# A Mamba block with a mixture of experts on one core: halves of channels added on GpSimd ahead of mean and variance, a reordered prologue, and a last store in two halves

## The chip, the cores and the metric

The kernel runs on one core of one Trainium2 chip. The metric is the device time of one execution in microseconds (us). Five engines work side by side and meet at semaphores: TensorE (PE in the profile), VectorE (DVE), ScalarE (ACT), GpSimd (POOL) and SyncE (SP, which only issues the DMAs here).

## What is computed

Four sequences of 256 positions with 256 channels go through two layers. Both are residual:

```python
x = x + ssm(ctx_1024, layernorm(x), ...)      # conv of 4 taps, silu, softplus, a scan over 256
                                              # positions with 16 states, gate silu(z)
x = x + ffn(layernorm(x), ...)
# in ffn, for all 1024 positions:
shared_out = sum(expert_apply(flat, w1, b1, w2, b2) for 2 shared experts) / 2
probs      = softmax(flat @ router_w + router_b)           # 32 experts, the 6 largest kept
routed_out = sum(g_e * expert_apply(flat, w1_e, b1_e, w2_e, b2_e) for all 32 experts)
# expert_apply: relu(x @ w1 + b1) @ w2 + b2, hidden width 176
# layernorm: (x - m) / sqrt(v + 1e-5), m and v over the 256 channels
```

All tensors are float32. The gates of experts that were not chosen are zero, so the kernel runs all 32 experts over all positions and multiplies by the gate.

## The kernel before

**Tiling.** A batch is one sequence, b = 0 to 3. Channels lie on the partitions in KD = 2 halves of 128 (k = 0, 1), positions along the free axis (L = 256). The hidden width of all experts is cut into NT = 47 tiles of 128 rows, taken in NP = 24 pairs (PAIRS; pair 1 is a single tile). For a pair the first layer is `z` (L546 to L548, twelve matmuls of two fp32r pieces each way), ScalarE applies bias and relu (L678), VectorE multiplies by the gate (`hg`, L853; L855 for the shared experts), and the second layer adds w2 times hg into the PSUM bank `acc` (L527), SKEW = 3 pairs later. In the profile an fp32 matmul leaves two records: "x8" at L527 is four matmuls. In batch 3 `hg` and w2 are split in two fp32r pieces (`split`), and the second layer of a pair is twelve matmuls.

**Staging.** While the 24 pairs of batch b run, the steps in front of and behind the scan of batch b+1 (table THIS) and the convolution, x_proj and dt of batch b+2 (table NEXT) are woven in. A table says beside which pair a step is issued; each engine goes through its own steps in the order of the pairs. On PE a step comes between the pair's first-layer matmuls and its second-layer matmuls, or behind the latter if its name is in BEHIND. The loop over batches is a hardware loop (Fori) for the first two, then written out. In front of pair 0 of batch 0 stands the prologue HEAD, a list of steps that every engine walks in this order and of which it takes its own. OPEN holds the steps beside pairs 0, 1 and 2 of batch 0.

**The steps that matter here.** `warm` is PE alone: n matmuls over a tile of ones (L448), some of them after a semaphore. `xin` (PE, L458), `cv0` (ACT), `taps` (DVE, L722; the range of taps stands in the name), `econv` (ACT), `uclip` (DVE), `usig` (ACT, two activations) and `u` (DVE, L738) give the convolved input u. `xall` is x_proj on PE (L467), written to `xdt`, which is the bank `dA[0]`; `dtl` (ACT, L605) copies it to `xd`, SP spills it to DRAM and loads it back spread over the partitions (`bc`, `bt`, `ct`); `dt` (PE), `sp` (ACT), `over`, `delta` (DVE) give the step width. Then come per state and half k: `bu` (POOL, L905), `decay` (ACT), `scan` and `prod` (DVE, L753 and L766), `fold` (POOL) or, in the prologue, `sum` (PE, L436, into `acc`). `ez1` to `ez3` (ACT) and `zmul` (DVE, L784) give the gate silu(z) in `sz`. `x1` (DVE, L794 to L799) is the residual. The second layernorm is `mean` (PE, L479: two matmuls with a matrix of 1/256, one for each half k, summed in PSUM), `centre` (DVE, L802), `sq` (ACT, L654), `var` (PE, L484, two matmuls), `r2` (ACT, L657 and L659), `norm` (DVE, L807 to L811, gives `xs`), `xh` (ACT) and `xl` (DVE) as its two pieces, `logits` (PE, L504), `top`, `ex`, `gates` (router) and `turn` (PE, L498, and ACT, L668: the gates transposed into `gT`). For batch 0 the gates of the first 16 experts are spread on chip: `spread` (PE, L490, into the bank `misc`; ACT, L665, copies it to `gt`). `w1h` (ACT, L574) and `w1l` (POOL, L888) split the first-layer weights in two pieces, in 12 chunks that SP loads into a ring of four (`stage`). `final` (DVE, L872) adds `acc` to the residual after a batch's last pair, and SP stores it (`store`, L352).

**Banks.** PSUM has z (4 banks), acc, dA[0], dA[1] and misc: all eight are in use. The transposed gates are written to misc, as is what `spread` writes; a copy out of misc has to be done before the next write.

```python
elif name == "turn":
    pe.wait_ge(S["g34_done"], b + 1)
    if first(b):
        pe.wait_ge(ld_g[0], 32)        # ACT's copy of the spread gates out of misc
```

## Time and profile before

| | us |
|---|---|
| median of 3 runs | 389.01 |
| the three runs | 388.66 to 389.68 |
| the profiled execution, as timed | 390.97 |
| its span in the trace | 389.2 |
| busy: PE / DVE / ACT / POOL | 360.5 / 260.1 / 216.8 / 196.2 |
| mean granted clock of TensorE | 0.968 of full |

The span runs from the first to the last event of the profiled execution. The granted clock is 1.00 or 0.50 for most stretches of the trace: 2.4 or 1.2 GHz. The time falls into a prologue (to about 66 us, with PE busy in part), the start of batch 0 (to about 93 us), and three and a half batches in which PE works without a pause, then the last store.

### The profile page before, as it was taken

The page shows a single profiled execution, that of the slowest core. Times are in us where ns is not written, and L with a number is a line of the kernel's source. Part 1 is how long each engine was busy: PE and PEld are TensorE (multiplying, and loading weights), DVE is VectorE, ACT ScalarE, POOL GpSimd, SP SyncE. Part 2 cuts the span into 40 slices and gives each one's busy share as a digit, 9 for nine tenths or more (in the row PEclk, how much of TensorE's full clock was granted, in tenths as well). Part 3 has the DMA queues.
Part 4 walks back from the last instruction along what each step waited for, and adds up shares of the span by engine and source line. Part 5 has one row for each costly group of instructions (what it writes and reads, how often), then busy time and mean ns, then how long its engine had stood idle before and what let it go on. Part 6 is the DMA issues. An engine that isn't in the chain of part 4 may idle for free.

```text
span 389.2 us, 6828 instructions
## 1 busy us (share of the span) xinstructions
PE 360.5 (93%) x2275; PEld 321.3 (83%) x2275; DVE 260.1 (67%) x449; ACT 216.8 (56%) x539; POOL 196.2 (50%) x152
## 2 busy tenths in 40 slices
PE   4646688899999999999999999999999999999996
PEld 2333466688999988999999889989999999999995
DVE  3379987579998547799877566799864534354443
ACT  2667765657764426477543445485523346565662
POOL 0479996078995002389852002799730024445442
PEclk9659899899999999999999999999999999999999
DMA  7397870169622324886322125974231244233320
GB/s 232 114 319 253 252 229 7 47 177 315 202 83 81 83 57 111 247 308 183 113 81 81 54 92 149 325 220 145 90 83 56 67 131 144 82 85 91 100 56 27
DMA packets 30735, 54.20 MB, mean 139 GB/s; under 512 B 3282, under 2 KB 8564, under 8 KB 30708
## 3 DMA queue, kind: packets, MB, share of 16 engines
q1 hardware_dynamic: 30708, 53.86, 45.5%
q8 instruction: 14, 0.23, 0.3%
q14 instruction: 13, 0.11, 0.1%
...
## 4 chain that ended last, share of the span: by engine, by line
PE 82%; DVE 9%; DMA 3%; issue 3%; ACT 1%; POOL 1%; DVEq 0%; POOLq 0%; SPq 0%; ACTq 0%
PE acc L527 39%; PE z L546 12%; PE z L548 11%; PE z L547 11%; DVE dA L753 5%; DMA bt<-bc 2%; PE z L448 2%; PE dA L467 1%; DMA bc<-xd 1%; PE acc L436 1%; PE acc L532 1%; PE misc L484 1%; PE misc L458 1%; PE misc L479 1%; DVE ya L766 1%
## 5 line engine op out<-in xcount | busy, mean ns | idle before, releaser
L527 PE MATMUL acc<-hg,w 128*128 128x256 f32 x564 | 133.6, 379 | 0.3 <-DVE hg L853 0.3
L678 ACT ACTIVATE z<-z,par 128x256 f32<-128x256 f32 x188 | 76.0, 440 | 99.3 <-PE z L548 99.2
L905 POOL TENSOR_TENSOR bu<-bt,du 128x512 f32<-128x512 f32 x64 | 81.1, 1279 | 86.0 <-DMA bt<-bc 58.8
L546 PE MATMUL z<-xh,w1l 128*128 128x256 f32 (+1 forms) x376 | 119.0, 316 | 0.3 <-DVE xl L815 0.3
L527 PEld LDWEIGHTS acc<-hg,w 128*128 128x128 f32 x564 | 102.4, 190 | 11.6 <-DVE hg L853 0.5
L853 DVE TENSOR_TENSOR hg<-z,gt 128x512 f32<-128x512 f32 x88 | 60.5, 688 | 74.0 <-ACT z L678 73.1
L548 PE MATMUL z<-xh,w1h 128*128 128x256 f32 (+1 forms) x376 | 106.5, 283 | 0.0
L547 PE MATMUL z<-xl,w1h 128*128 128x256 f32 (+1 forms) x376 | 106.2, 283 | 0.0
L753 DVE TENSOR_TENSOR_SCAN dA<-dA,bu 128x512 f32<-128x512 f32 x64 | 78.2, 1222 | 9.9 <-POOL bu L905 9.4
L546 PEld LDWEIGHTS z<-xh,w1l 128*128 128x128 f32 x376 | 71.4, 190 | 6.7 <-issue 4.7
L547 PEld LDWEIGHTS z<-xl,w1h 128*128 128x128 f32 x376 | 71.0, 189 | 1.6
L548 PEld LDWEIGHTS z<-xh,w1h 128*128 128x128 f32 x376 | 70.9, 189 | 0.0
L913 POOL TENSOR_TENSOR ya<-ya,pr 128x512 f32<-128x512 f32 x42 | 53.9, 1282 | 22.7 <-DVE pr L766 22.0
L926 POOL TENSOR_TENSOR w2l<-w,w2h 128x512 fp32r<-128x512 f32 (+1 forms) x24 | 31.3, 1304 | 64.1 <-ACT w2h L685 64.1
L626 ACT ACTIVATE dA<-delta,aneg 128x255 f32<-128x255 f32 x128 | 55.0, 462 | 0.0
L766 DVE TENSOR_TENSOR pr<-dA,ct 128x512 f32<-128x512 f32 x50 | 34.6, 692 | 6.1 <-DVE dA L753 0.5
L888 POOL TENSOR_TENSOR w1l<-stage,w1h 128x1024 fp32r<-128x1024 f32 (+1 forms) x12 | 27.5, 2323 | 13.9 <-ACT w1h L574 13.9
L623 ACT ACTIVATE dA<-zeros 128x2 f32<-128x2 f32 x64 | 11.1, 173 | 36.7 <-DVE pr L766 27.8
L527 PE MATMUL acc<-hh,w2h 128*128 128x256 f32 x94 | 26.5, 282 | 0.0
L527 PE MATMUL acc<-hh,w2l 128*128 128x256 f32 x94 | 26.5, 282 | 0.0
L527 PE MATMUL acc<-hl,w2h 128*128 128x256 f32 x94 | 26.4, 281 | 0.0
L436 PE MATMUL acc<-pr,par 128*128 128x256 f32 x32 | 10.7, 475 | 11.1 <-DVE pr L766 11.1
...
## 6 DMA issues: line engine op xcount, KB each, us to landing
w<-in_w SPq DMA_DIRECT2D x92, 256.0 KB, 2.8
bt<-bc SPq DMA_DIRECT2D x32, 256.0 KB, 4.9
ct<-bc SPq DMA_DIRECT2D x32, 256.0 KB, 5.6
...
gt<-gates SPq DMA_DIRECT2D x14, 128.0 KB
xr<-in_xr SPq DMA_DIRECT2D x4, 256.0 KB, 5.7
x<-in_xT SPq DMA_DIRECT2D x4, 256.0 KB, 4.3
out<-x SPq DMA_DIRECT2D x4, 256.0 KB, 4.7
```

What stands on the lines that cost most here:

```text
L527: mm = pe.matmul(acc[:, k, :], weights, h, start=t + k + n == 0, stop=last, skip_group_check=True)
L546: pe.matmul(z[p % ZB][:, i, :], w1l[:, t, one], xh_, start=k == 0, stop=False)
L547: pe.matmul(z[p % ZB][:, i, :], w1h[:, t, one], xl_, start=False, stop=False)
L548: mm = pe.matmul(z[p % ZB][:, i, :], w1h[:, t, one], xh_, start=False, stop=k == KD - 1)
L626: ins = act.activation(dA[k][:, j, 1:L], delta[:, k, 1:L], ACT.Exp, scale=aneg[:, n:n + 1])
L678: ins = act.activation(z[p % ZB][:, i, :], z[p % ZB][:, i, :], ACT.Relu, bias=b1[:, t:t + 1])
L753: dve.tensor_tensor_scan(flat(dA[k]), flat(dA[k]), bu[:, (c * KD + k) % BURING, :], 0.0, ALU.mult, ALU.add).then_inc(S["scan_done"], 1)
L766: dve.tensor_tensor(products(b, c)[:, k, :], flat(dA[k]), flat(ct[:, c % BRING]), ALU.mult).then_inc(S["prod_done"], 1)
L853: ins = dve.tensor_tensor(hg[:, p % 4], z[p % ZB][:], gt[:, 2 * half:2 * half + 2, :], ALU.mult)
L905: pool.tensor_tensor(bu[:, r, :].rearrange("p (j l) -> p j l", j=2), bt[:, c % BRING], du[:, k:k + 1, :].broadcast_to([P, 2, L]), ALU.mult ...
L913: pool.tensor_tensor(ya[:, k, :], ya[:, k, :], pr[:, k, :], ALU.add).then_inc(S["y_folded"], 1)
L926: pool.tensor_tensor(w2l[:, p % 4, 0:n, :], w2[:, p % RING, 0:n, :], w2h[:, p % 4, 0:n, :].bitcast(F32), ALU.subtract).then_inc(S["w2l_don ...
```

## The change

It has six parts.

1. **Mean and variance, batches 1 to 3.** GpSimd adds the two channel halves of x1 (`x1s`, beside pair 18) and of the squares (`sqs`, beside pair 19) into free quarters of `ya`; `mean` and `var` are then one matmul each instead of two. `mean` moves from behind the second layer of pair 18 to ahead of that of pair 19; `var` moves from ahead of the second layer of pair 20 to behind it. Batch 0 keeps its two matmuls.
2. **Spread gates in acc.** `spread` writes to acc, which is free until the second layer of batch 0 begins, instead of misc; `turn` no longer waits for the copy; a new step `acc_free` has PE wait for the copy after the first layer of pair 2. `spread` and `turn` move from pair 2 to pair 1.
3. **x_proj of batch 1 ahead of pair 0.** `xall` and `dtl` move from behind pair 0 into the prologue, between the logits and pair 0; `dt`, `sp`, `over`, `delta` move from pair 1 to pair 0. On the way `taps`, `econv`, `uclip`, `usig` and `u` of batch 1 each move forward, and the last `w1h`/`w1l` moves back behind the logits.
4. **zmul of batch 0 on GpSimd**, at chunk 6 of the prologue's scans; `ez3` writes to SBUF (`ez`, which is `cv`) instead of misc, and `cv0` of batch 1 now waits for that zmul.
5. **Warm matmuls.** 16 more behind the first xin, 8 instead of 6 behind uclip, and 22, 13 and 31 instead of 14, 8 and 24 around mean and var of batch 0.
6. **The end.** In batch 3 the second layer's half k = 1 goes to the bank dA[0] instead of acc. The last pair does all of k = 0 first. VectorE adds and SP stores each half by itself.

```diff
-BACK = [("yfold", 16), ("x1", 17), ("mean", 18), ("centre", 19), ("sq", 19), ("var", 20), ("r2", 20), ("norm", 20), ("logits", 21),
+BACK = [("yfold", 16), ("x1", 17), ("x1s", 18), ("mean", 19), ("centre", 19), ("sq", 19), ("sqs", 19), ("var", 20), ("r2", 20), ("norm", 20), ("logits", 21),
...
-BEHIND = ("mean", "logits", "xall", "dt", "turn")
+BEHIND = ("var", "logits", "xall", "dt", "turn")
...
-HEAD = [(("warm", None, 11), 0), ("xin", 0), ("cv0", 0), (("taps", 1, KC), 0), (("warm", "conv_done", 6), 0), ("econv", 0), ("uclip", 0),
-        (("warm", "uclip_done", 6), 0), ("usig", 0), ("w1h", 0), ("w1l", 0), (("warm", "usig_done", 4), 0), ("u", 0), ("stats", 0), ("xall", 0),
+HEAD = [(("warm", None, 11), 0), ("xin", 0), (("warm", None, 16), 0), ("cv0", 0), (("taps", 1, KC), 0), (("warm", "conv_done", 6), 0), ("econv", 0), ("uclip", 0),
+        (("warm", "uclip_done", 8), 0), ("usig", 0), ("w1h", 0), ("w1l", 0), (("warm", "usig_done", 4), 0), ("u", 0), ("stats", 0), ("xall", 0),
...
-    HEAD += [(n, 0) for n in ((), (), ("zz",), ("ez1",), ("ez2",), ("ez3",), (), ())[_c]]
+    HEAD += [(n, 0) for n in ((), (), ("zz",), ("ez1",), ("ez2",), ("ez3",), ("zmul",), ())[_c]]
...
-         (("warm", None, 14), 0), ("w1h", 0), ("zmul", 0), ("x1", 0), ("mean", 0), (("warm", None, 8), 0), (("taps", 1, 2), 1),
-         ("centre", 0), ("sq", 0), ("w1l", 0), (("taps", 2, KC), 1), ("var", 0), ("w1h", 0), ("w1l", 0), ("r2", 0), ("econv", 1),
-         (("warm", None, 24), 0), ("norm", 0), ("uclip", 1), ("xh", 0), ("logits", 0), ("usig", 1), ("xl", 0), ("top", 0),
-         ("ex", 0), ("u", 1), ("gates", 0)]
-OPEN = [[("xall", 1), ("dtl", 1)],
-        [("dt", 1), ("sp", 1), ("over", 1), ("delta", 1)],
-        [("spread", 0), ("turn", 0)] +
+         (("taps", 1, 2), 1), (("warm", None, 22), 0), ("w1h", 0), ("x1", 0), ("mean", 0), (("warm", None, 13), 0), (("taps", 2, 3), 1),
+         ("centre", 0), ("sq", 0), ("w1l", 0), (("taps", 3, KC), 1), ("var", 0), ("econv", 1), ("uclip", 1), ("r2", 0),
+         (("warm", None, 31), 0), ("norm", 0), ("usig", 1), ("xh", 0), ("logits", 0), ("w1h", 0), ("w1l", 0), ("u", 1), ("xl", 0),
+         ("top", 0), ("ex", 0), ("xall", 1), ("gates", 0), ("dtl", 1)]
+OPEN = [[("dt", 1), ("sp", 1), ("over", 1), ("delta", 1)],
+        [("spread", 0), ("turn", 0)],
+        [("acc_free", 0)] +
...
+        x1s, sqs = ya[:, 0, 0:L], ya[:, 1, 0:L]
...
+        def final_batch(b):
+            return type(b) is int and b == B - 1
+
+        def total(b, k):
+
+            return dA[0][:, 0, :] if k and final_batch(b) else acc[:, k, :]
...
-            store(B - 1)
-            eng.wait_ge(S["stored"], 16 * (B + 1))
+            eng.wait_ge(S["half_added"], 1)
+            eng.dma_start(out_d[:, 0, B - 1, :], x1[:, (B - 1) % 2, 0, :]).then_inc(S["stored"], 16)
+            eng.wait_ge(S["ot_done"], B + 1)
+            eng.dma_start(out_d[:, 1, B - 1, :], x1[:, (B - 1) % 2, 1, :]).then_inc(S["stored"], 16)
+            eng.wait_ge(S["stored"], 16 * (B + 2))
...
-                    pe.wait_ge(S["x1_done"], b + 1)
-                    for k in range(KD):
-                        mm = pe.matmul(misc[:, 0, :], meanw[:], x1[:, b % 2, k, :], start=k == 0, stop=k == KD - 1)
+                    if first(b):
+                        pe.wait_ge(S["x1_done"], 1)
+                        for k in range(KD):
+                            mm = pe.matmul(misc[:, 0, :], meanw[:], x1[:, 0, k, :], start=k == 0, stop=k == KD - 1)
+                    else:
+                        pe.wait_ge(S["x1_halved"], b)
+                        mm = pe.matmul(misc[:, 0, :], meanw[:], x1s, start=True, stop=True)
                     mm.then_inc(S["mean_done"], 1)
                 elif name == "var":
...
-                    pe.wait_ge(S["sq_done"], b + 1)
-                    for k in range(KD):
-                        mm = pe.matmul(misc[:, 0, :], meanw[:], sq[:, k, :], start=k == 0, stop=k == KD - 1)
+                    if first(b):
+                        pe.wait_ge(S["sq_done"], 1)
+                        for k in range(KD):
+                            mm = pe.matmul(misc[:, 0, :], meanw[:], sq[:, k, :], start=k == 0, stop=k == KD - 1)
+                    else:
+                        pe.wait_ge(S["sq_halved"], b)
+                        mm = pe.matmul(misc[:, 0, :], meanw[:], sqs, start=True, stop=True)
                     mm.then_inc(S["var_done"], 1)
...
-                            mm = pe.matmul(misc[:, g, t * P:(t + 1) * P], wide[:, t, g * P:(g + 1) * P], ident,
+                            mm = pe.matmul(acc[:, g, t * P:(t + 1) * P], wide[:, t, g * P:(g + 1) * P], ident,
...
+                elif name == "acc_free":
+                    pe.wait_ge(ld_g[0], 32)
...
-                    if first(b):
-                        pe.wait_ge(ld_g[0], 32)
...
-                for i, t in enumerate(PAIRS[p]):
-                    for k in range(KD):
+                order = [(i, k) for i in range(len(PAIRS[p])) for k in range(KD)]
+                if final_batch(b) and p == NP - 1:
+                    order = [(i, k) for k in range(KD) for i in range(len(PAIRS[p]))]
+                for i, k in order:
+                        t = PAIRS[p][i]
                         one = slice(k * P, (k + 1) * P)
...
-                            mm = pe.matmul(acc[:, k, :], weights, h, start=t + k + n == 0, stop=last,
+                            mm = pe.matmul(total(b, k), weights, h, start=t + n == 0 and (k == 0 or final_batch(b)), stop=last,
                                            skip_group_check=True)
+                            if last and final_batch(b) and k == 0:
+                                mm.then_inc(S["half_done"], 1)
...
-                        act.wait_ge(S["ez_done"], b)
+                        act.wait_ge(S["zmul_done" if type(b) is int and b == 1 else "ez_done"], b)
...
-                    act.activation(misc[:], ez[:], ACT.Exp, scale=-1.0).then_inc(S["ez_done"], 1)
+                    act.activation(ez[:] if first(b) else misc[:], ez[:], ACT.Exp, scale=-1.0).then_inc(S["ez_done"], 1)
...
-                    act.activation(gt[:, 0:2, :], misc[:], ACT.Copy).then_inc(ld_g[0], 32)
+                    act.activation(gt[:, 0:2, :], acc[:], ACT.Copy).then_inc(ld_g[0], 32)
...
-                elif name == "zmul":
+                elif name == "zmul" and not first(b):
...
-            final(B - 1)
+            e = (B - 1) % 2
+            dve.wait_ge(S["half_done"], 1)
+            dve.tensor_tensor(x1[:, e, 0, :], total(B - 1, 0), x1[:, e, 0, :], ALU.add).then_inc(S["half_added"], 1)
+            dve.wait_ge(S["l2_done"], B * NP)
+            dve.tensor_tensor(x1[:, e, 1, :], total(B - 1, 1), x1[:, e, 1, :], ALU.add).then_inc(S["ot_done"], 1)
...
+                elif name == "zmul" and first(b):
+                    pool.wait_ge(S["ez_done"], 1)
+                    pool.tensor_tensor(sz[:], sz[:], ez[:], ALU.mult).then_inc(S["zmul_done"], 1)
...
+                elif name == "x1s":
+                    pool.wait_ge(S["y_folded"], b * NC * KD)
+                    pool.wait_ge(S["x1_done"], b + 1)
+                    pool.tensor_tensor(x1s, x1[:, b % 2, 0, :], x1[:, b % 2, 1, :], ALU.add).then_inc(S["x1_halved"], 1)
+                elif name == "sqs":
+                    pool.wait_ge(S["sq_done"], b + 1)
+                    pool.tensor_tensor(sqs, sq[:, 0, :], sq[:, 1, :], ALU.add).then_inc(S["sq_halved"], 1)
```

**PE in the prologue**, from the sum over the last states to the first layer of pair 0. `ones` are the warm matmuls, `par,ya` the logits, `dA<-u,par` is x_proj. Before:

```order
L436 MATMUL acc<-ya,par 128x256 x4
L448 MATMUL z<-ones 128x256 x14
L479 MATMUL misc<-x,meanw 128x256 x2
L448 MATMUL z<-ones 128x256 x8
L484 MATMUL misc<-pr,meanw 128x256 x2
L448 MATMUL z<-ones 128x256 x24
L504 MATMUL misc<-par,ya 128x32 x4
L546 MATMUL z<-xh,w1l 128x256
```

and now:

```order
L447 MATMUL acc<-ya,par 128x256 x4
L459 MATMUL z<-ones 128x256 x22
L491 MATMUL misc<-x,meanw 128x256 x2
L459 MATMUL z<-ones 128x256 x13
L500 MATMUL misc<-pr,meanw 128x256 x2
L459 MATMUL z<-ones 128x256 x31
L523 MATMUL misc<-par,ya 128x32 x4
L478 MATMUL dA<-u,par 40x256 x2
L570 MATMUL z<-xh,w1l 128x256
```

x_proj stands between the logits and the first layer, and the three groups of warm matmuls are longer.

**VectorE at the same place**, from the end of x1 to the logits. `cv<-z,par,cv` are the taps of batch 1, `e<-e` is uclip, `u<-cv,e` is u. Before:

```order
L799 TENSOR_TENSOR x<-dA,x 128x512
L722 SCALAR_TENSOR_TENSOR cv<-z,par,cv 128x255 x2
L802 TENSOR_TENSOR dA<-x,misc 128x512
L722 SCALAR_TENSOR_TENSOR cv<-z,par,cv 128x254 x2
L722 SCALAR_TENSOR_TENSOR cv<-z,par,cv 128x253 x2
L807 SCALAR_TENSOR_TENSOR z<-misc,pr 128x256
L808 TENSOR_TENSOR z<-z,pr 128x256
L809 TENSOR_SCALAR z<-z 128x256
L810 TENSOR_TENSOR pr<-z,pr 128x256
L811 TENSOR_TENSOR ya<-dA,pr 128x2x256
L731 TENSOR_SCALAR e<-e 128x512
L815 TENSOR_TENSOR xl<-ya,xh 128x512
```

and now:

```order
L823 TENSOR_TENSOR x<-dA,x 128x512
L746 SCALAR_TENSOR_TENSOR cv<-z,par,cv 128x254 x2
L826 TENSOR_TENSOR dA<-x,misc 128x512
L746 SCALAR_TENSOR_TENSOR cv<-z,par,cv 128x253 x2
L755 TENSOR_SCALAR e<-e 128x512
L831 SCALAR_TENSOR_TENSOR z<-misc,pr 128x256
L832 TENSOR_TENSOR z<-z,pr 128x256
L833 TENSOR_SCALAR z<-z 128x256
L834 TENSOR_TENSOR pr<-z,pr 128x256
L835 TENSOR_TENSOR ya<-dA,pr 128x2x256
L762 TENSOR_TENSOR u<-cv,e 128x512
L839 TENSOR_TENSOR xl<-ya,xh 128x512
```

The first tap went ahead of x1, uclip ahead of the norm, and u stands between the norm and xl.

**PE around var in the loop**, from the last first-layer matmuls of pair 20 to x_proj of the batch after next. Before:

```order
L548 MATMUL z<-xh,w1h 128x256
L484 MATMUL misc<-pr,meanw 128x256 x2
L513 REGISTER_ALU
L527 MATMUL acc<-hg,w 128x256 x4
L464 ISA
L465 REGISTER_ALU
L467 MATMUL dA<-u,par 40x256 x2
```

and now:

```order
L572 MATMUL z<-xh,w1h 128x256
L532 REGISTER_ALU
L549 MATMUL acc<-hg,w 128x256 x4
L503 MATMUL misc<-ya,meanw 128x256
L475 ISA
L476 REGISTER_ALU
L478 MATMUL dA<-u,par 40x256 x2
```

var is one matmul over `ya` and stands behind the second layer.

## Rows read from the trace of the kernel before

**Rows 1.** Busy by stretch: PE, PEld, DVE, ACT, POOL, granted clock, DMA share, GB/s.

```profile
93.00:169.00 76.00, 76.00 (x473) 69.10 (x472) 57.07 (x101) 41.73 (x114) 35.98 (x31) 1.00 0.48 147
```

**Rows 2.** The chain that ended last, in order of time: start us, us, what.

```profile
129.30 0.86 PE misc L479 x4
131.60 1.73 PE acc L527 x8
134.77 0.86 PE misc L484 x4
137.36 0.99 PE dA L467 x4
```

**Rows 3.** Timeline of that layernorm: start us, us, engine, line, operation, [idle before].

```profile
127.74 0.69 DVE L799 TENSOR_TENSOR x<-dA,x 128x512 f32 x1 [0.21 <-DVE dA L798]
133.81 0.60 ACT L654 ACTIVATE pr<-dA 128x512 f32<-128x512 f32 x1 [1.36 <-DVE dA L802]
136.63 0.42 DVE L807 SCALAR_TENSOR_TENSOR pr<-misc,pr 128x256 f32<-128x256 f32 x1 [0.28 <-ACT pr L659]
138.33 0.69 DVE L811 TENSOR_TENSOR ya<-dA,pr 128x512 f32<-128x512 f32 x1
```

**Rows 4.** Groups by line and shape, POOL: busy us, mean ns, idle before.

```profile
L917 POOL TENSOR_TENSOR pr<-ya 128x256 f32<-128x256 f32 x6 | 4.3, 739 | 0.0
```

**Rows 5.** Timeline, from the last state sum of batch 0 to its third pair.

```profile
54.04 1.13 PE L436 MATMUL acc<-ya,par 128*128 128x256 f32 x4 [0.27 <-DVE ya L766]
64.94 1.08 PE L504 MATMUL misc<-par,ya 128*128 128x32 f32 x8 [0.97 <-DVE ya L811]
65.58 0.69 DVE L815 TENSOR_TENSOR xl<-ya,xh 128x512 fp32r<-128x512 f32 x1 [0.36 <-ACT xh L662]
66.33 0.39 PE L546 MATMUL z<-xh,w1l 128*128 128x256 f32 x1 [0.31 <-DVE xl L815]
66.97 0.53 ACT L672 ACTIVATE ex<-lg,nm 128x32 f32<-128x32 f32 x2 [0.24 <-DVE nm L825]
68.66 1.92 PE L467 MATMUL dA<-u,par 128*40 128x256 f32 x4
70.61 0.38 ACT L605 ACTIVATE xd<-dA 40x256 f32<-40x256 f32 x1 [1.03 <-PE dA L467]
76.10 0.60 PE L498 MATMUL misc<-par,g 128*34 128x128 f32 x4 [1.04 <-ACT gt L665]
76.63 0.38 PE L546 MATMUL z<-xh,w1l 128*128 x1
```

**Rows 6.** The chain, columns as in Rows 2: the fourth second layer of batch 0.

```profile
87.24 1.99 PE acc L527 x8
```

**Rows 7.** Busy time by stretch, columns as in Rows 1: the granted clock around pair 0.

```profile
67.00:68.00 1.00, 1.00 (x7) 1.00 (x6) 0.94 (x7) 0.51 (x2) 0.00 (x0) 0.51 0.00 0
```

**Rows 8.** Timeline, the last pair and the last store.

```profile
381.78 1.33 POOL L926 TENSOR_TENSOR w2l<-w,w2h 128x512 fp32r<-128x512 f32 x1 [1.54 <-ACT w2h L685]
382.32 1.33 DVE L867 TENSOR_TENSOR hl<-hg,hh 128x512 fp32r<-128x512 f32 x1 [0.37 <-ACT hh L692]
385.51 0.69 DVE L872 TENSOR_TENSOR x<-acc,x 128x512 f32<-128x512 f32 x1 [1.86 <-PE acc L527]
386.23 0.59 SPq L352 DMA_DIRECT2D out<-x  x1
```

**Rows 9.** DMA issues by line: count, KB each, median us to landing.

```profile
w<-in_w SPq DMA_DIRECT2D x92, 256.0 KB, 2.8
w<-in_w SPq DMA_DIRECT2D x4, 128.0 KB, 2.1
```

**Rows 10.** Timeline, warm matmuls at either clock, and a wait for a weight chunk.

```profile
9.82 3.57 PE L448 MATMUL z<-ones 128*128 128x256 bf16 x16 [4.10 <-DVE cv L722]
57.25 1.06 ACT L574 ACTIVATE w1h<-stage 128x1024 fp32r<-128x1024 f32 x1 [1.32 <-DMA stage<-in_w]
61.18 2.78 PE L448 MATMUL z<-ones 128*128 128x256 bf16 x24
```

6 lines of the change are left out of this document (3 added, 3 removed).

## Prediction

> **What bounds the kernel now.** I read the busy time by stretch first. From 93 us to the last second layer PE is busy in every microsecond at a granted clock of 1.00, 76.00 of 76.00 us in the first such stretch, while VectorE, ScalarE and GpSimd have gaps [rows 1]. So what takes matmul time out of that part shortens the kernel by as much, as long as no new wait opens on PE. Then comes the chain that ended last, in order of time: its loop part is PE alone. Before 93 us PE waits for others, and there the timeline tells which wait ends last. The profiled span of 389.2 stands beside a median of 389.01 for the three runs, so I take the terms off the median; the profiled execution's own 390.97 lies 1.8 above its span, and I assume nothing about that. 0.3% of this time, 1.2 us, is what a measurement can tell from no change.
>
> **Part 1, mean and var in batches 1 to 3.** Two fp32 matmuls of 256 columns take 0.86 us at mean and 0.86 at var [rows 2]. One of each two goes: 0.43 x 2 x 3 = 2.58 us, all in the stretch where PE never rests.
> The adds cost GpSimd 0.74 each by its own add of the same size [rows 4], six in all; they count only if PE comes to mean or var too early. The pieces: a second layer is 1.73, a pair's first layer 131.60 - 130.16 = 1.44 [rows 2]. x1 is there at 128.43 [rows 3], plus 0.74 is 129.2. The new mean comes after the first layer of pair 19, at 129.30 + 1.44 = 130.7: 1.5 us in hand. The squares end at 134.41 [rows 3]; they hang on relu and gate of pair 19, whose first layer now comes 0.86 earlier, so 133.6, plus 0.74 is 134.3. The new var stands at 130.7 + 0.43 + 1.73 + 1.44 + 1.73 = 136.1: 1.8 in hand.
> What is tighter is behind var. From its end (134.77 + 0.86 = 135.63) to xs (138.33 + 0.69 = 139.02) the chain over ScalarE and the norm on VectorE takes 3.39 us [rows 2, 3]. PE now has between var and the logits x_proj 0.99, one first layer 1.44 and one second layer 1.73 [rows 2], 4.16 in all, so 0.8 in hand in batches 1 and 2. In batch 3 there is no x_proj: 3.17, a wait of 0.22. The part brings 2.58 - 0.22 = **2.4 us**. Its bounds are 2.6, and 1.1 if each batch loses 0.5 to waits.
>
> **Parts 2 and 3, the start of batch 0.** Now the logits end at 66.02, PE waits 0.31 for xl, the first pair takes from 66.33 to 68.66, x_proj 1.92, and `xd` is there at 70.99. Later PE waits 1.04 for the copy of the spread gates, and pair 3 begins at 76.63 [rows 5]. In the middle of this the granted clock is at 0.51, half speed [rows 7]; x_proj takes 0.99 at full speed [rows 2].
> On the data side: u of batch 1 is pulled ahead of xl, into the 0.36 that VectorE idles there plus what the moved uclip leaves free [rows 5]; u and xl therefore end at about 65.6 and 66.3, and xl is not late. x_proj runs from 66.0 to 67.0 if the clock holds. On ScalarE ex (66.97 + 0.53 = 67.50) stands ahead of the copy, 0.38 [rows 5], so xd is there at 67.9 instead of 71.0: 3.1 us earlier. The DRAM round trip, bu and the scans hang on it and move with it. SP's queue has nothing new in front.
> On PE: pair 0 starts at 67.0, not 66.33. Behind it stand two first layers of 1.44 each (pairs 0 and 2), one of half that (pair 1), dt, the spread at about 1.05 and the turn at 0.6 [rows 2, 5], without the wait. With 1.1 for dt that is 67.0 + 2.9 + 0.7 + 1.1 + 1.05 + 0.6 = 73.4 against 76.63, again about 3.1. Of this 1.04 is the wait, 0.31 the filled gap before pair 0, and the rest half clock that is gone. acc_free is met by then: the copy ends near 73. The gate of pair 3, queued on VectorE behind the first scans, held PE only just (0.29 at 87.24, [rows 6]); both sides move by the same 3.1, so that stays. The part brings **3.1 us**. If the clock falls here as before, pair 0 and what follows loses half of up to 3.4 us, and the part brings 1.5.
> For the clock, first the row: it fell at 67 us [rows 7] after PE had stood idle for 0.97 ahead of the logits and 0.31 behind them [rows 5]. The change fills the first gap with seven warm matmuls more, the second with x_proj. By the Trainium skill ("TensorE: Matmul & The Clock Gate", Part 1) the engine is throttled by default and sustained activity releases it; by that rule the fall should be gone. The sum by the rule is the 3.1 above, and without it 1.5.
>
> **Part 4, zmul on GpSimd.** It takes 0.68 us off VectorE, but x1 waited for the last state sum on PE, which ends at 54.04 + 1.13 [rows 5], so nothing is gained. It puts about 1.3 us (twice 0.74 less overhead) on GpSimd, in front of six weight chunks: each ring slot comes free later, SP issues one of the last two chunk loads 1.3 later, and ScalarE, which waited for a chunk at 57.25 [rows 10], waits until about 58.5 and is done at 59.6, just when `sq` is due. Taken at nothing; it would cost up to 0.5 if that load is slow. cv0 of batch 1 waits for zmul, but its tap stands behind the last scans anyway.
>
> **Part 5, warm matmuls.** At full clock one costs 2.78 / 24 = 0.116, at half 3.57 / 16 = 0.22 [rows 10]. At full clock 22, 13 and 31 of them take 2.5, 1.5 and 3.6 us, which just fits the gaps. So they cost nothing there. The 16 behind the first xin stand in a wait and might have the clock up for the first x_proj (0.9 us, bounds 0 and 0.9); since the waits behind them stay, I take 0.
>
> **Part 6, the end.** The last add (0.69, [rows 8]) becomes two of 256 columns, 0.42 each by the nearest row [rows 3]; the first hides under the six last matmuls (0.7 us), so 0.27 is saved. The last store is then 128 instead of 256 KB; loads of these sizes land 2.1 and 2.8 us after issue [rows 9], so 0.7 less at most, minus a little for the half before it in flight: 0.6. The part brings **0.9 us**, bounds 0.3 and 1.3. The second bank costs no matmul.
>
> **Sum.** 2.4 + 3.1 + 0 + 0 + 0.9 = 6.4; 389.0 - 6.4 = **382.6 us**.
>
> **The rivals.** (a) The clock still falls around pair 0. The rows show that it does so under a PE busy most of the time. Then parts 2 and 3 bring 1.5: 384.2 us. The same time comes out if the three timed runs did not have the fall that the profile shows. (b) The clock is up for the first x_proj as well: 381.7. (c) The loop's matmul time comes back as waits for the longer chain (x1, add, mean, and square, add, var). Against it speak the 1.5 and 1.8 us in hand; with half of it back, 384.0 to 385.0. (d) GpSimd's adds hold VectorE up, or the other way round. The row: a two-operand subtract on VectorE took 1.33 us instead of 0.69 while a GpSimd add ran from 381.78 to 383.11 [rows 8]. So the two do block each other; here sqs meets `u` (both operands in SBUF) and sets it back by up to 0.74, while u has slack. If all six landed on PE's path it would cost 6 x 0.74 = 4.4: 387.0 us. The Trainium skill ("SBUF — State Buffer", on the shared port pair) has such pairs exclude each other for a whole instruction; by that rule the row is explained, and it speaks against any add on GpSimd beside VectorE. (e) Slower than before: the clock is down while the longer warm groups run. 66 of them at 0.22 take 14.5 instead of 7.7 us, and mean, var and logits behind them double, 1.5 more; less some 1 us of gap that is 7.3 us onto the chain, and the start of batch 0 then gains 1.5 only: 384.2 + 7.3 = 391.5. It decides against the change once about 5 us are lost, that is when some two thirds of 55 to 65 us run at 1.2 GHz. Against it: the profile has 1.00 there at the old, sparser filling.
>
> **How the numbers follow.** 382.6 holds 50%; (a) 24%; (b) 8%; (c) 8%; (d) 3%; (e) 3%; the rest 4% lies between. Range 381.5 to 385.0: it takes in (b), (a) and most of (c). Faster by over 0.3% is everything but (e) and a little rest: 95%. Within 0.3%: 2%. Slower: 3%.
>
> **What would show it.** mean and var as one matmul of 0.43 each, PE without idle from about 90 us, a wait of about 0.2 before the logits of batch 3 alone. xd of batch 1 at 68 instead of 71, pair 3 at 73.5, no wait between spread and turn, the clock at 1.00 from 66 to 71. The last add at 0.4 and a span that ends about 2.3 us behind it. It is wrong if warm groups run past x1 or sq, if ScalarE's chunk wait reaches past 59.6, or if VectorE's gate (hg) comes late in the first ten pairs of batch 0.

## The result, and the profile after

The kernel after takes 386.38 us, the median of 22 runs (383.06 to 391.40), beside 389.12 us for the kernel before (22 runs, 387.56 to 391.30). The ratio is 0.990, with a 95% interval of 0.988 to 0.992; the ratios here and below leave out the runs of after at 389 us and over (five of these 22) and none of the kernel before. So the change is faster, by 3.9 us of the ratio and 2.7 us of the medians (2.5 us by the means of all 22 runs of each), where I had forecast 6.4. The median lies above my range of 381.5 to 385.0, and the two figures differ because the runs of after stand in groups, near 384 (eight of them up to 384.8), near 387 and near 391. That spread turned out to be the main finding.

The profiled execution took 384.17 us, with a span of 382.4. Its page begins:

```profile
span 382.4 us, 6892 instructions
...
PE 358.6 (94%) x2301; PEld 320.4 (84%) x2301; DVE 261.6 (68%) x449; ACT 216.7 (57%) x539; POOL 201.9 (53%) x159
...
PE 84%; DMA 5%; DVE 5%; POOL 3%; ACT 2%; issue 1%; SPq 0%; DVEq 0%; POOLq 0%; ACTq 0%
```

**The loop** did what was forecast. The timeline of batch 1, and of batch 3 (start us, us, engine, line, operation, [idle before]):

```profile
126.69 0.60 PE L494 MATMUL misc<-ya,meanw 128*128 128x256 f32 x2
...
128.94 0.69 DVE L762 TENSOR_TENSOR u<-cv,e 128x512 f32<-128x512 f32 x1
...
129.74 0.73 POOL L956 TENSOR_TENSOR ya<-pr 128x256 f32<-128x256 f32 x1 [4.13 <-ACT pr L678]
...
293.68 0.59 PE L503 MATMUL misc<-ya,meanw 128*128 128x256 f32 x2
...
297.72 1.08 PE L523 MATMUL misc<-par,ya 128*128 128x32 f32 x8 [0.28 <-DVE ya L835]
```

Where [rows 2] had four matmuls for mean and four for var (an fp32 matmul is two records), two are left. `u` keeps its 0.69 and has ended (129.63) when GpSimd's add of the squares starts (129.74). The two never run side by side here, so these rows can't show whether they would hold each other up. PE's one wait in the loop is 0.28 us, before batch 3's logits. From 93 to 169 us PE is busy throughout, as in [rows 1].

**The end**, beside [rows 8] and [rows 9]:

```profile
378.90 0.42 DVE L903 TENSOR_TENSOR x<-acc,x 128x256 f32<-128x256 f32 x1 [1.16 <-PE acc L549]
...
379.61 0.42 DVE L905 TENSOR_TENSOR x<-dA,x 128x256 f32<-128x256 f32 x1 [0.28 <-PE dA L549]
...
380.06 0.34 SPq L436 DMA_DIRECT2D out<-x  x1
```

The last add takes 0.42 instead of 0.69, and the span ends 2.34 us behind the last issue instead of 2.97.

**The start of batch 0** went otherwise. The timeline of ScalarE, VectorE and GpSimd:

```profile
50.80 1.25 POOL L927 TENSOR_TENSOR sz<-sz,cv 128x512 f32<-128x512 f32 x1
...
57.99 1.06 ACT L598 ACTIVATE w1h<-stage 128x1024 fp32r<-128x1024 f32 x1 [2.05 <-DMA stage<-in_w]
...
58.96 0.58 ACT L678 ACTIVATE pr<-dA 128x512 f32<-128x512 f32 x1
...
60.09 1.52 DVE L755 TENSOR_SCALAR e<-e 128x512 f32<-128x512 f32 x1 [0.95 <-ACT e L616]
...
65.73 1.82 POOL L916 TENSOR_TENSOR w1l<-stage,w1h 128x768 fp32r<-128x768 f32 x1 [1.90 <-ACT w1h L598]
...
66.14 1.44 DVE L849 TENSOR_SCALAR nm<-m 128x2 f32<-128x2 f32 x1
...
67.62 0.53 ACT L696 ACTIVATE ex<-lg,nm 128x32 f32<-128x32 f32 x2 [1.96 <-DVE nm L849]
```

The same clip (`e`) and the same `nm` in the kernel before:

```profile
64.81 0.42 DVE L731 TENSOR_SCALAR e<-e 128x512 f32<-128x512 f32 x1
...
66.77 0.17 DVE L825 TENSOR_SCALAR nm<-m 128x2 f32<-128x2 f32 x1
```

Three things are to be seen. The chunk wait that was 1.32 us [rows 10] is 2.05, and behind it the squares (L678) start at 58.96, though the centred x was there at 58.37. The clip of the conv exponent (L755) takes 1.52 instead of 0.42. And an instruction on 256 numbers (`nm`, L849) takes 1.44 us instead of 0.17, just while GpSimd subtracts the last low half of w1; `ex` waits 1.96 us for it. The granted clock is 1.00 from 53 to 76 us, the spread and the turn stand without a wait between them, and `xd` is there at 68.42.

### The profile page after: what moved, and what is told of

The parts are those of the page before. It is cut to its first block, busy times and chain, and to the rows that moved or that the text cites. A ratio compares the mean times of both kernels' runs of the same rounds, so it can differ in the third digit from the quotient of the medians.

```text
span 382.4 us, 6892 instructions
## 1 busy us (share of the span) xinstructions
PE 358.6 (94%) x2301; PEld 320.4 (84%) x2301; DVE 261.6 (68%) x449; ACT 216.7 (57%) x539; POOL 201.9 (53%) x159
## 4 chain that ended last, share of the span: by engine, by line
PE 84%; DMA 5%; DVE 5%; POOL 3%; ACT 2%; issue 1%; SPq 0%; DVEq 0%; POOLq 0%; ACTq 0%
PE acc L549 36%; PE z L570 12%; PE z L571 12%; PE z L572 12%; PE dA L549 4%; DMA bt<-bc 3%; PE acc L447 2%; DVE dA L777 1%; POOL w1l L916 1%; PE acc L556 1%; POOL bu L936 1%; PE misc L469 1%; DMA stage<-in_w 1%; PE dA L483 1%; PE dA L478 1%
## 5 line engine op out<-in xcount | busy, mean ns | idle before, releaser
L447 PE MATMUL acc<-pr,par 128*128 128x256 f32 x32 | 12.3, 526 | 11.4 <-DVE pr L790 11.4
L447 PEld LDWEIGHTS acc<-pr,par 128*128 128x128 f32 x32 | 7.2, 247 | 15.9 <-DVE pr L790 15.1
L459 PE MATMUL z<-ones 128*128 128x256 bf16 x123 | 16.1, 285 | 4.1 <-DVE cv L746 2.4
L459 PEld LDWEIGHTS z<-ones 128*128 128x128 bf16 x123 | 12.3, 102 | 7.4 <-issue 3.7
```

## The experiments

All against runs of the kernel before on the same chip; the ratio has its 95% interval.
"After, old warm" is the kernel after with the old warm groups, and "without the start" is the change without its new start of batch 0.

```
kernel            median us (range, runs)          before    ratio
loop alone        387.13 (385.85 to 388.66, 12)    388.88    0.9947 [0.9923, 0.9972]
end alone         388.91 (387.09 to 390.26, 12)    388.88    0.9986 [0.9961, 1.0011]
warm alone        387.31 (386.73 to 387.68, 12)    388.88    0.9941 [0.9917, 0.9964]
after, old warm   388.79 (386.48 to 390.73, 12)    388.88    0.9974 [0.9947, 1.0001]
product back      384.22 (383.61 to 384.53,  6)    388.48    0.9884 [0.9851, 0.9918]
low half late     383.51 (382.99 to 387.95,  6)    388.48    0.9875 [0.9834, 0.9917]
these two         383.75 (382.34 to 384.76,  6)    388.48    0.9869 [0.9832, 0.9906]
padded before     388.23 (387.21 to 390.00, 12)    388.48    0.9988 [0.9961, 1.0016]
after again       386.69 (383.19 to 390.12,  6)    388.91    0.9881 [0.9834, 0.9927]
clip from PSUM    383.77 (382.80 to 384.62,  6)    388.91    0.9862 [0.9833, 0.9891]
all three mends   382.68 (382.19 to 383.71,  6)    388.91    0.9842 [0.9814, 0.9870]
without the start 384.41 (384.22 to 386.75,  6)    388.91    0.9890 [0.9857, 0.9923]
```

### The parts by themselves

**The loop alone**: the kernel before with the adds on GpSimd and one matmul each for mean and var.

```
-                    for k in range(KD):
-                        mm = pe.matmul(misc[:, 0, :], meanw[:], x1[:, b % 2, k, :], start=k == 0, stop=k == KD - 1)
+                        pe.wait_ge(S["x1_halved"], b)
+                        mm = pe.matmul(misc[:, 0, :], meanw[:], x1s, start=True, stop=True)
...
+                    pool.tensor_tensor(x1s, x1[:, b % 2, 0, :], x1[:, b % 2, 1, :], ALU.add).then_inc(S["x1_halved"], 1)
```

> The kernel before with part 1 alone (x1s and sqs on GpSimd, mean and var as one matmul in batches 1 to 3). If my working of the loop holds: 2.58 us of matmul time go, 0.2 to 0.3 come back as one wait in batch 3, so 2.3 us less than before, ratio 0.994. If the shortfall of the changed kernel (3.9 us gained where 6.4 were forecast) lies in the loop: under 1 us less, and idle of PE in front of mean or var or the logits in batches 1 and 2.

It takes 2.1 us off by the ratio. In its trace the stretch between the same two second layers is 19.94 us in batches 1 and 2 where the kernel before has 20.80, and 28.37 in batch 3 where it has 28.64: 0.86 + 0.86 + 0.27 = 2.0 us.

**The end alone**: the last halves one by one.

```
-            final(B - 1)
+            dve.wait_ge(S["half_done"], 1)
+            dve.tensor_tensor(x1[:, e, 0, :], total(B - 1, 0), x1[:, e, 0, :], ALU.add).then_inc(S["half_added"], 1)
+            dve.wait_ge(S["l2_done"], B * NP)
+            dve.tensor_tensor(x1[:, e, 1, :], total(B - 1, 1), x1[:, e, 1, :], ALU.add).then_inc(S["ot_done"], 1)
```

> The kernel before with part 6 alone (last halves singly, second bank). Working: 0.9 us less, ratio 0.9977, the last VectorE add 0.42 instead of 0.69 and the end of the span 2.3 us behind it instead of 3.0. If two stores in flight hinder each other: 0.3 us less or nothing.

The time is 0.5 us less by the ratio, with no change inside the interval. In the trace the stretch from the issue of the last batch's gates to the end is 76.2 us instead of 77.1. The forecast 0.9 is borne out by the trace and neither shown nor refuted by the times.

**The warm groups alone**: the kernel before with the counts of the change.

```
-HEAD = [(("warm", None, 11), 0), ("xin", 0), ("cv0", 0), (("taps", 1, KC), 0), (("warm", "conv_done", 6), 0), ("econv", 0), ("uclip", 0),
+HEAD = [(("warm", None, 11), 0), ("xin", 0), (("warm", None, 16), 0), ("cv0", 0), (("taps", 1, KC), 0), (("warm", "conv_done", 6), 0), ("econv", 0), ("uclip", 0),
```

> The kernel before with the longer warm groups alone (part 5). Theory 1: 1 to 2 us slower than before in the median, with single runs up to 393. Rival: within 0.5 us of before; where the clock is held up around pair 0 even 1 us faster.

**After with the old warm groups**: the reverse edit, in all five groups.

```
-         (("taps", 1, 2), 1), (("warm", None, 22), 0), ("w1h", 0), ("x1", 0), ("mean", 0), (("warm", None, 13), 0), (("taps", 2, 3), 1),
+         (("taps", 1, 2), 1), (("warm", None, 14), 0), ("w1h", 0), ("x1", 0), ("mean", 0), (("warm", None, 8), 0), (("taps", 2, 3), 1),
```

> The changed kernel with the warm matmuls of the kernel before (no 16 behind xin, 6, 14, 8, 24). Theory 1 (the longer warm groups cost time whenever the clock is at 1.2 GHz in the prologue, since they then outlast the gap that they fill): the slowest times at 389 to 391 us and 0.965 mean clock disappear and the median falls from 386 to about 384.5. Rival (the shortfall sits in GpSimd's zmul and weight chunk, not in the warm groups): the median stays within 0.5 us of the changed kernel or rises by up to 1.5, since the clock falls around pair 0 as before.

I had feared that the longer groups cost. They bring 2.3 us by the ratio on top of the kernel before, and without them the change as a whole keeps only 1.0 of its 3.9. Both results lie outside every range written down beforehand: the theory that the groups cost is refuted, and its rival had the direction right and the size too small. One part of the gain can be seen in the traces: the first x_proj is shorter, and the matmul behind it starts at 14.48 us with the warm groups alone, where the five profiles with the old groups have it at 14.98 to 15.72. Of the two timelines the first is of the end alone, with the old groups, the second of the warm groups alone:

```profile
9.89 3.57 PE L458 MATMUL z<-ones 128*128 128x256 bf16 x16 [4.10 <-DVE cv L737]
13.39 1.50 PE L477 MATMUL dA<-u,par 128*40 128x256 f32 x4
15.36 1.12 PE L482 MATMUL dA<-xd,par 8*128 8x256 f32 x4 [0.47 <-ACT xd L620]
```

```profile
12.26 0.60 PE L448 MATMUL z<-ones 128*128 128x256 bf16 x4 [0.29 <-ACT e L599]
12.99 1.03 PE L467 MATMUL dA<-u,par 128*40 128x256 f32 x4
14.48 1.13 PE L472 MATMUL dA<-xd,par 8*128 8x256 f32 x4 [0.47 <-ACT xd L605]
```

The other part goes with the clock. Of 35 runs of the kernel before, the 15 with the lowest mean granted clock (0.963 to 0.969) took 389.4 to 391.4 us, the 20 others 387.7 to 389.5. The profile that I forecast from was of the first kind (390.97 us, 0.968). Those of the loop alone and the end alone were of the second (0.982), and in them the clock fall at 67 us [rows 7] is absent. With the longer groups all twelve runs lie between 386.7 and 387.7, with a mean clock of 0.976 and more, and the profiled one has no fall at 67 us. So it is likely, and not shown, that the slower runs of the kernel before are those with that fall. The mean clock doesn't say where the clock was low: the profiles of after again (below) and of the product back both have 0.977, the first with a fall to 0.50 at 67 to 70 us, the second with none there. And the larger part of the distance from 0.968 to 0.982 lies between 9 and 16 us, where the view gives 0.50 for the kernel before and 1.00 for the loop alone although their 16 warm matmuls take the same 3.57 us.

Loop, end and groups together make 2.1 + 0.5 + 2.3 = 4.9 us by ratios and 3.3 by medians, more than the 3.9 and 2.7 of the whole change. So the new start of batch 0, from which I expected 3.1, seems to bring nothing or worse; the kernel without it, below, measures this directly.

### What the new start runs into

**The product back on VectorE**, as in the kernel before.

```
-                elif name == "zmul" and not first(b):
+                elif name == "zmul":
...
-                elif name == "zmul" and first(b):
-                    pool.wait_ge(S["ez_done"], 1)
-                    pool.tensor_tensor(sz[:], sz[:], ez[:], ALU.mult).then_inc(S["zmul_done"], 1)
```

> The kernel after, with the first batch's gate product z*sigmoid(z) back on VectorE in its 0.7 us slot before x1, as in the kernel before. Theory Z (the product on GpSimd is on the path: behind it stand the w1 halves, then a load of the stage ring, then ScalarE's copy, which ends 0.6 us after the centred x is there): the squares start 0.5 to 0.7 us earlier, the x_proj copy of batch 1 too, and the time falls from about 386.4 by 0.5 to 0.9, to 385.5 to 385.9. Rival (the product is hidden, as I forecast, and the prologue is bound elsewhere): 386.4 within 0.3, or 0.3 slower for the 0.7 us on VectorE.

The step also goes back to its old place ahead of `x1`, and `ez3` writes to misc again. The squares start at 58.35 us and the copy of x_proj at 67.45, both 0.6 earlier than in the first profile of after. That looks like theory Z, but a second profile of after (after again, below), with the product still on GpSimd, has

```profile
57.44 1.06 ACT L598 ACTIVATE w1h<-stage 128x1024 fp32r<-128x1024 f32 x1 [2.03 <-DMA stage<-in_w]
58.41 0.58 ACT L678 ACTIVATE pr<-dA 128x512 f32<-128x512 f32 x1
```

The squares stand there only 0.17 us behind the centred x (58.24). In the kernel without the new start, with the product on VectorE, they stand 1.14 behind it (59.08 and 57.94). So how late that chunk comes differs from profile to profile, and that the product delays the squares is not shown. The time fell by 2.2 us against after's median of 386.4, more than the 0.5 to 0.9 of theory Z, and all six runs lie within 0.9 us. What else had changed is the clip (L755): 0.64 us here. It was issued at 59.48, 0.3 us ahead of the end of one of GpSimd's subtractions.

**The last low half held back**, so that GpSimd is idle while VectorE works on the logits.

```
                     pool.wait_ge(w1h_done, i + 1)
+                    if i == NW - 1:
+                        pool.wait_ge(S["sp_done"], 2)
```

> The kernel after, with GpSimd's last piece of w1's low half held back until ScalarE's softplus of batch 1 is done (about 71.8 us instead of 65.7), where VectorE has only adds and products of two tensors. Theory P (VectorE's small tensor_scalar of 256 numbers, 1.44 us instead of 0.17, is stopped by the GpSimd subtraction beside it): that instruction is back at 0.17 to 0.2 us, ex starts 1.2 to 1.3 us earlier, the x_proj copy with it, PE's wait of 0.46 us before the dt product goes, and the time falls by 0.4 to 0.5 us, to about 386.0. Rival (the clock or the order on PE decides and not this instruction): the small instruction stays at over 1 us, or it falls and PE starts the dt product at 68.4 all the same; 386.4 within 0.3.

**Both edits**, the two diffs above in one kernel.

> Both edits: the product back on VectorE, and the last low half held back. If theories Z and P both hold and are apart in time, the gains add: 0.5 to 0.9 and 0.4 to 0.5, so 1.0 to 1.4 us below the kernel after, 385.0 to 385.4, and about 4.9 us below the kernel before. Rival (both only fill the same slack): no more than the larger of the two alone, 385.6 to 386.0.

The small instruction is back at 0.17 us in both, so theory P holds for it, and PE's wait before the dt product is gone too. But the medians do not add up as expected: 383.51 us where 386.0 was expected, and 383.75 where it was 385.0 to 385.4. The profiled run with the low half late alone took 387.95 us, over 4 us above most of its others. Its timeline:

```profile
59.44 3.52 DVE L755 TENSOR_SCALAR e<-e 128x512 f32<-128x512 f32 x1 [0.70 <-ACT e L616]
...
65.47 1.73 PE L523 MATMUL misc<-par,ya 128*128 128x32 f32 x8 [2.31 <-DVE ya L835]
```

The clip takes 3.52 us here, the norm chain behind it (in program order on VectorE) is late, and PE waits 2.31 us for `ya`. In the kernel before the clip stood behind that chain, at 64.81 us. With both edits the clip took 2.24 us, and PE waited 1.02. So there was a third cause, with an outcome that differs from run to run.

**After again, and the clip from PSUM.** The fourth edit lets ScalarE write the exponent into the PSUM bank of batch 1's input projection, free by then, and VectorE read it there.

```
-                    act.activation(e1[:], cv[:], ACT.Exp, scale=-1.0).then_inc(S["econv_done"], 1)
+                    act.activation(xin(b)[:] if type(b) is int and b == 1 else e1[:], cv[:], ACT.Exp, scale=-1.0).then_inc(S["econv_done"], 1)
...
-                    dve.tensor_scalar(e1[:], e1[:], BIG, 1.0, ALU.min, ALU.add).then_inc(S["uclip_done"], 1)
+                    dve.tensor_scalar(e1[:], xin(b)[:] if type(b) is int and b == 1 else e1[:], BIG, 1.0, ALU.min, ALU.add).then_inc(S["uclip_done"], 1)
```

> The kernel after once more, beside the three that follow, so that they can be set against it. Theory U: its runs spread from 383 to 391 us because the clip of batch 1's conv exponent on VectorE (L755), which the change moved ahead of the layernorm's chain, is issued while GpSimd's back-to-back subtractions of w1 run: it comes through either at the next boundary between two of them or only behind the last, so it takes 0.4, 1.5 or up to 3.6 us, and in the long case PE's warm group runs out and the clock falls. The runs should again lie between 383 and 391 with at least two clusters, the median between 384.5 and 386.5. Rival (something of that day's chip made the spread): all within 1.5 us of each other.

> The kernel after, but ScalarE writes batch 1's conv exponent into PSUM (the bank of its input projection, free by then) and VectorE's clip reads it there. Theory U: the clip then never waits for GpSimd and takes 0.6 to 0.8 us in place of 0.4, 1.5 or 3.6; the runs above 386 go, all lie within about 1.5 us, and the median is that of the fast cluster of the kernel after, 384.0 to 384.6. Rival (the spread has its cause elsewhere, in the clock itself): the clip is short but the spread and the runs at 389 to 391 stay, and the median is that of the kernel after.

After again took 383.19, 383.55, 386.60, 386.77, 389.39 and 390.12 us: three groups, with a median 0.2 us above the range expected. This time the profile caught one of the middle runs (386.77). First its chain that ended last, in order of time, then GpSimd's timeline, then the busy time by stretch (columns as in [rows 1]):

```profile
59.05 0.64 ACT e L616
...
59.71 3.68 DVE e L755
63.39 0.35 DVE z L831
...
65.16 0.70 DVE ya L835
...
65.90 1.19 PE misc L523 x8
67.09 1.86 PE dA L478 x4
```

```profile
51.49 11.61 POOL L916 TENSOR_TENSOR w1l<-stage,w1h 128x1024 fp32r<-128x1024 f32 x5
67.32 1.80 POOL L916 TENSOR_TENSOR w1l<-stage,w1h 128x768 fp32r<-128x768 f32 x1 [4.22 <-ACT w1h L598]
```

```profile
66.00:67.00 1.00, 1.00 (x8) 0.96 (x8) 0.90 (x2) 1.00 (x2) 0.00 (x0) 0.86 0.00 0
67.00:68.00 1.00, 1.00 (x4) 0.51 (x4) 0.92 (x6) 0.25 (x1) 0.68 (x1) 0.50 0.08 16
...
69.00:70.00 1.00, 1.00 (x5) 1.00 (x6) 0.87 (x9) 0.80 (x3) 0.13 (x1) 0.50 0.00 0
```

GpSimd does five subtractions of 2.32 us back to back, from 51.49 to 63.10; one of them ends at about 60.8. The clip is issued at 59.71 and ends at 63.39, that is 0.3 us behind the last of them: it was passed over at 60.8. PE's 31 warm matmuls end at 63.55, PE waits 2.35 us for `ya` ahead of the logits, the clock falls to 0.50, and x_proj takes 1.86 us (1.93 in the timeline) instead of the 1.06 in the timeline of the first profile. In the first profile of after the clip was issued at 60.09 and ended at 61.61, at a boundary between two subtractions. In the six profiles in which the clip reads SBUF at this place it took 0.64, 1.52, 2.24, 3.52, 3.64 and 3.68 us (the product back, after, the two edits together, the low half late, after with the old warm groups, after again), and each time it ended 0.1 to 0.3 us behind a boundary: in the first three behind the next one, in the last three behind the one after, with which the row of subtractions ended.

With the operand in PSUM it takes its 0.69 us beside the same subtractions:

```profile
59.80 0.69 DVE L755 TENSOR_SCALAR e<-z 128x512 f32<-128x512 f32 x1 [0.94 <-ACT z L616]
```

All six runs then lie between 382.8 and 384.6, and none of the groups near 387 and 390 is left. The median is 0.2 us below the range expected and the spread 1.8 us instead of 1.5; theory U holds. No profile caught a run of after near 390: that those runs owe their time to the clip rests on their absence here alone. The Trainium skill has this as a rule: by "SBUF — State Buffer", section "SBUF: two separate sides", a VectorE instruction in a mode that uses both read ports and a GpSimd instruction exclude each other for a whole instruction, and by "VectorE: DVE Perf Modes", section "Why PSUM operands drop a tier", an operand in PSUM keeps an instruction out of that mode. The traces agree with both: 0.42 us alone and up to 3.68 blocked from SBUF, 0.69 and not blocked from PSUM in both profiles that have it there. The three waits of over 3 us are longer than one subtraction, since the clip was passed over at one boundary.

**All three mends together**: the product back, the low half late and the clip from PSUM.

> The kernel after with three edits: the clip reads PSUM, the product z*sigmoid(z) is back on VectorE, the last low half is held back until the softplus. If the three causes are apart: the fast cluster at 384.2, less 0.6 for the product and 0.45 for the small tensor_scalar, so 383.0 to 383.4, with no run above 385. Rival (once the clip is free the others only fill slack): 384.0 to 384.4.

382.68 us, 6.2 us below the kernel before on that chip by the medians and 1.58% by the ratio, 0.3 below the range expected: the fastest version of the study. It lies 1.1 us below the clip from PSUM alone, as the expected 0.6 and 0.45 together would have it; the runs of the two overlap, and which edit brings what is not shown. The small instruction takes 0.17, `ex` starts at 64.83, the copy of x_proj at 65.27, and PE has no wait from 64 us on until its pairs run.

**Without the new start**: the kernel before with loop, end and warm groups. Beside the two diffs of the loop and the end:

```
-         (("warm", None, 24), 0), ("norm", 0), ("uclip", 1), ("xh", 0), ("logits", 0), ("usig", 1), ("xl", 0), ("top", 0),
+         (("warm", None, 31), 0), ("norm", 0), ("uclip", 1), ("xh", 0), ("logits", 0), ("usig", 1), ("xl", 0), ("top", 0),
```

> The kernel before with the halves added by GpSimd, the single last halves and the longer warm groups, and without the new start of batch 0 (x_proj of batch 1 behind pair 0 as before, the spread in its old bank, the product on VectorE, the clip behind the layernorm). By the parts alone (2.06, 0.5 and 1.6 us below the kernel before) it should stand 4.2 us below it, near 384.5 to 385.0. Theory J (the new start as built brings about as much as its two blocked instructions and the product cost): no more than 1 us above the fast cluster of the kernel after (384.2) and below its median. Rival (the parts overlap, and the new start carries the whole change, as I forecast with 3.1 us of 6.4): 386.5 or more.

384.41 us, 4.3 below the kernel before by the ratio, where the parts alone make 4.9. That is near the fastest group of the kernel after, and 2.3 us below the median that after has on the same chip. The runs of after again set beside it are 1 us faster in the best two and 2 to 6 us slower in the other four; so as built the new start gives 1 us at best and more often costs. Mended it gives 384.41 - 382.68 = 1.7 us. One of the six runs without the new start took 386.75 us at a mean clock of 0.977, though its clip stands behind the norm: a run can also come out over 2 us long for a cause that no profile here caught.

### A fetch in the way of a transfer

In the kernel before, and in the two kernels with only the loop or only the end, batch 1's B and C rows land late after their spill to DRAM. The timeline of the loop alone, and its DMA between 69.0 and 70.5 and between 70.5 and 72.3 us (queue, kind: packets, MB, share):

```profile
68.48 0.33 SPq L331 DMA_DIRECT2D bc<-xd  x1
72.24 0.33 SPq L341 DMA_DIRECT2D bt<-bc  x1
...
77.52 1.23 DVE L762 TENSOR_TENSOR_SCAN dA<-dA,bu 128x512 f32<-128x512 f32 x1 [3.26 <-POOL bu L914]
```

```profile
q1 hardware_dynamic: 45, 0.03, 7.7%
q8 instruction: 1, 0.02, 3.9%
...
q1 hardware_dynamic: 3, 0.00, 1.0%
```

The load of `bt` is issued 3.76 us after the spill, since 3 of the spill's 48 packets come over a microsecond behind the others, and in between stands one packet of the queue "instruction". In the kernel after this packet is at 66.1 us, ahead of the spill at 68.44, and the load follows in 1.52 us. In the kernel before it is at 72.1, and the spill lands 3.4 us after its issue. In the kernel after with the old warm groups it is at 74 us, behind the spill at 70.50, and the load again follows in 1.5 us.

**The kernel before, padded** with 42 matmuls of 8 columns between the state sums, which only lengthen PE's instruction stream.

```
                 if name[0] == "sum":
+                    for _ in range(6 * (name[1] < NC - 1)):
+                        pe.matmul(z[0][:, 0, 0:8], ones[:, 0:P], ones[:, 0:8], start=True, stop=True)
                     sum_states(name[1])
```

> The kernel before, with 42 matmuls of 8 columns between the state sums of batch 0, which do nothing but lengthen PE's instruction stream by some 84 instructions ahead of the first pair. In the kernel before the trace shows one instruction packet of PE's queue at 72.1 us, in the middle of the spill of batch 1's B and C rows, which lands 3.4 us after its issue instead of 1.5; in the kernel after it is at 66.1 us, ahead of the spill, which lands in 1.5. Theory F (the fetch holds back part of the spill, and the longer warm groups of the change moved it out of the way): the packet comes 5 to 8 us earlier, the spill lands in 1.5 us, VectorE's wait before batch 1's first scan falls from about 3 us to 1.3, PE's wait for hg (0.3 to 0.8) goes, and the time falls by 0.4 to 0.8 us. Rival (the late landing has another cause, and the gain of the longer warm groups is all in the clock): the spill still lands after 3.4 us or more, and the time is that of the kernel before within 0.3.

The packet moved to 62 us, and the spill landed in time:

```profile
68.90 0.33 SPq L330 DMA_DIRECT2D bc<-xd  x1
70.42 0.33 SPq L340 DMA_DIRECT2D bt<-bc  x1
...
75.96 1.23 DVE L755 TENSOR_TENSOR_SCAN dA<-dA,bu 128x512 f32<-128x512 f32 x1 [1.28 <-ACT dA L628]
```

The scan's wait fell from 3.26 (2.74 in the profile of before) to 1.28 us, and PE's wait for `hg` (0.29 in [rows 6], 0.81 in the loop alone) is gone. So theory F holds for the mechanism. The time, 0.3 us less by the medians with an interval from -1.5 to +0.6 us, can't tell its 0.4 to 0.8 us from nothing. The Trainium skill ("Runtime: NRT & Kernel Launch", section "Instruction fetch mechanics") has instructions fetched in blocks of 16 KiB (256 instructions) over a queue of the engine's own, the cost mostly hidden. The trace agrees with the size: the queue moves 0.23 MB in 14 packets. PE has no wait beside the packet, but the transfer is held up.

## Why the prediction was wrong, step by step

The direction and the bound were right: PE in the loop, waits and the clock ahead of it. The time missed because of the base that one term was taken off, and because of two steps that I put at nothing or thought free.

**The clock fall that I took for the rule.** The step that failed is "I take the terms off the median" for parts 2 and 3. Their 3.1 us was read between rows of one execution whose clock had fallen at 67 us [rows 7]; that run stood at 390.97, 1.9 us above the median, and the text says that it assumes nothing about that. It set the span of 389.2 beside a median of 389.01 and took them as equal, but a run's time is 1.8 us above its span in every profile here (384.17 and 382.4 in the kernel after), so the profiled run was no median run. One measure shows what was in it: the time from the start of the squares to the first second layer of batch 0, by the timelines.

```
before, the profiled run (clock 0.50 at 67 to 70)     59.57 to 78.16   18.6 us
end alone (clock 1.00 there)                          58.91 to 75.95   17.0
loop alone                                            58.58 to 75.63   17.1
warm alone                                            58.25 to 75.29   17.0
padded before                                         59.00 to 76.05   17.1
without the new start                                 59.08 to 76.10   17.0
after, first profile                                  58.96 to 74.86   15.9
after again, the clip at 3.68                         58.41 to 77.45   19.0
product back, the clip at 0.64                        58.35 to 74.26   15.9
these two, the clip at 2.24                           58.35 to 74.55   16.2
low half late, the clip at 3.52                       58.00 to 78.56   20.6
after, old warm groups, the clip at 3.64              58.83 to 78.92   20.1
clip from PSUM                                        58.70 to 74.60   15.9
all three mends                                       57.43 to 72.82   15.4
```

My forecast for after was 18.6 - 3.1 = 15.5, and the mended kernel does it in 15.4. But all five kernels with the old order there, profiled without the fall, need 17.0 to 17.1, so 1.5 us of the 3.1 was a fall that not every run has. Beside 17.1 the term of 3.1 measures 1.2 in the kernel after at its best (15.9) and 1.7 mended (15.4); where the clip is passed over it is a loss of 1.9 to 3.5 (19.0 to 20.6). The kernel before itself was profiled only once, so that its own usual run needs 17.1 is taken over from its near copies. Rival (a) named just this, with 384.2 us and 24%, though I took the other value for the likeliest. The best group of after's runs stands at 384.

**"u of batch 1 is pulled ahead of xl, into the 0.36 that VectorE idles there plus what the moved uclip leaves free."** The prediction counts what the moved clip frees at 64.8 and not what it meets at 59.5. There GpSimd subtracts w1 without a pause. I had the mechanism in rival (d), with a row of it [rows 8] (the GpSimd instruction in that row is a subtract, not an add), and looked for it only where the change adds work to GpSimd. There it didn't happen, since `sqs` and `u` don't meet; it lay where the change moves VectorE's work beside GpSimd's. I priced a block at 0.74 us; it was up to 3.3 (3.68 less 0.42), and the clock fall behind it came on top.

**The last low half.** The change issues it behind the logits, where it runs into `nm`: 1.26 us on ScalarE's chain, of which PE sees 0.46. The prediction does not mention it.

**Part 4 at nothing.** The working was right up to its last step: "waits until about 58.5 and is done at 59.6, just when `sq` is due". The 59.6 was that of the slow profile. In the first profile of after the wait lasted to 57.99 and the squares were due at 58.37, so they came 0.6 us late, near the "up to 0.5 if that load is slow". In after again they came only 0.2 late, and as said above it is not shown that the product is the reason.

**Part 5 at nothing, and rival (b).** The groups bring 2.3 us by the ratio (1.6 by the medians). The first x_proj was indeed at full clock in all nine profiles with the 16 early matmuls, at 1.03 us (rival (b), 8%), and what hangs on it starts 0.5 to 1.2 us earlier than in the profiles without them, near its bound of 0.9. The rest goes with the runs of low mean clock, which are gone. I treated the groups as a cost to be bounded, and gave the missing fall to parts 2 and 3. How much of the early gain arrives at the squares of batch 0 is open: they start at 58.96 and 58.41 us in the two profiles of after, at 58.25 with the warm groups alone and at 58.58 with the loop alone.

**Part 1.** 2.0 us where 2.4 was forecast. In batches 1 and 2 it is exactly the 0.86 each, and the slack of 0.8 to 1.8 held. The wait before batch 3's logits was forecast at 0.22 and is 0.28. What I had not counted is about 0.3 us more there: eight small matmuls that start from idle take 1.08 instead of 0.97, and they can't start beside the end of the matmuls ahead of them.

**Part 6.** The trace shows the 0.9; the times can't tell.

**Rivals (c) and (e)** did not happen: no wait but the one of 0.28 opened in the loop, and in the profile of after the clock stood at 1.00 through the long groups. The fall of rival (a) is gone in that profile, as expected of the filled gaps, but it stands in after again at 67 to 70 us, behind the gap of 2.35 us that the late clip opens. What the range left out was that a run of the same kernel might differ from the next by 7 us. It had no case in which the median lies between two groups of runs.

Added up with what was measured, from the runs of the kernel before with a mean clock above 0.969 (388.3, their median): 2.0 for the loop, 0.9 for the end and 1.2 for the stretch from the squares to the second layer (17.1 less 15.9) make 4.1, and the resulting 384.2 is the best group of after. Its median lies 2 us above. That the runs near 387 owe their place to the clip is shown by one profile among them and by their absence once the clip reads PSUM. For those near 390, whose mean clock (0.965 to 0.968) is lower than that profile's 0.977, only their absence speaks.
